# A four-layer conditional kernel: one identity add moved from VectorE to GpSimd, one load moved to ScalarE's queue, three warm-up matmuls fewer

## The reference

```
x = x + einsum('bct,bcd->bdt', x, W0[c15])        # L0: 16 matrices of 64 x 64, one picked per batch
x = x + einsum('bct,bcd->bdt', x, W1[c15])        # L1: the same form, the same condition
x = x + x @ W2.T + 0.5 * (x @ A[c2]) @ B.T        # L2: 1024 x 1024, with a low-rank part of rank 32
x = x + x @ W3[c7].T                              # L3: one of 8 matrices of 1024 x 1024 per batch
```

## Time and profile before

| | |
|---|---|
| runs | 385.03, 385.55, 385.63 us |
| the profiled execution's own time | 385.22 us |
| its span, from the first to the last instruction | 383.4 us |
| mean granted TensorE clock | 0.998 |
| TensorE busy | 377.7 us, 98% |
| VectorE busy | 269.2 us, 70% |
| ScalarE busy | 224.4 us, 59% |
| GpSimd busy | 117.8 us, 31% |

### The profile page before, as it was taken

How to read it: one execution, slowest core, us unless ns; L and a number is a source line. 1 busy time by engine, 2 the same in 40 slices (tenths; PEclk the granted TensorE clock), 3 DMA queues, 4 the chain that set the end, 5 groups by cost and what they waited for, 6 DMA issues and landing times.

```text
span 383.4 us, 7702 instructions
## 1 busy us (share of the span) xinstructions
PE 377.7 (98%) x1760; PEld 315.2 (82%) x1761; DVE 269.2 (70%) x300; ACT 224.4 (59%) x299; POOL 117.8 (31%) x157
## 2 busy tenths in 40 slices
PE   8999999999999999999999999999999999999995
PEld 8888888888888888888888888888888888888784
DVE  3796978856849788537869468963599626989643
ACT  3679558496246476245475465753677546778433
POOL 0000140100000000024766346753268532576500
PEclk9999999999999999999999999999999999999999
DMA  8975904640368384406427315552256522663223
GB/s 271 398 288 175 372 3 150 224 172 5 110 237 287 134 322 136 173 29 218 147 88 233 94 32 191 194 168 59 55 208 206 142 58 58 220 217 119 60 64 85
DMA packets 24187, 61.38 MB, mean 160 GB/s; under 512 B 1906, under 2 KB 2098, under 8 KB 24114
## 3 DMA queue, kind: packets, MB, share of 16 engines
q1 hardware_dynamic: 23792, 60.37, 47.3%
q10 hardware_dynamic: 322, 0.18, 0.2%
HBM read 52.15 MB, written 8.39 MB: 158 GB/s over the span
## 4 chain that ended last, share of the span: by engine, by line
PE 99%; POOL 0%; ACT 0%; issue 0%; ACTq 0%; POOLq 0%
PE ps L1496 45%; PE ps L1364 12%; PE ps L1363 12%; PE ps L1365 12%; PE ps L1390 4%; PE ps L1519 4%; PE ps L1429 3%; PE ps L1584 2%; PE ps L1402 2%; PE ps L1335 1%; PE ps L1343 1%; PE ps L1534 0%; POOL st L452 0%; ACT stage L841 0%; ACTq L840 0%
## 5 line engine op out<-in xcount | busy, mean ns | idle before, releaser
L1496 PE MATMUL ps<-ring,aT 128*128 x752 | 173.4, 389 | 0.0
L1496 PEld LDWEIGHTS ps<-ring,aT 128*128 128x128 f32 x752 | 141.0, 188 | 29.8 <-issue 0.7
L1364 PE MATMUL ps<-ring 128*128 128x512 f32 x208 | 81.0, 389 | 0.0
L1363 PE MATMUL ps<-ring 128*128 128x512 f32 x208 | 81.0, 389 | 0.0
L1365 PE MATMUL ps<-ring 128*128 128x512 f32 x208 | 80.9, 389 | 0.0
L471 POOL TENSOR_TENSOR aT<-xT,aT 128x512 fp32r<-128x512 f32 (+1 forms) x36 | 56.2, 1581 | 45.8 <-ACT aT L754 40.3
L1246 DVE TENSOR_TENSOR ring<-raw,ring 128x1024 f32 (+1 forms) x40 | 64.1, 1659 | 6.2 <-ACT ring L740 6.2
L760 ACT ACTIVATE aT<-ps 64x1024 fp32r<-64x1024 f32 x32 | 32.7, 1021 | 47.6 <-PE ps L1496 47.2
L1274 DVE TENSOR_TENSOR stage<-ps,stage 64x1024 f32<-64x1024 f32 x30 | 36.7, 1222 | 27.5 <-ACT stage L769 26.8
L1263 DVE TENSOR_TENSOR aT<-ps,aT 64x1024 fp32r<-64x1024 f32 x32 | 39.1, 1222 | 21.6 <-ACT aT L760 20.9
L1365 PEld LDWEIGHTS ps<-ring 128*128 128x128 f32 x208 | 39.0, 188 | 8.1
(11 more groups left out here) (94 smaller groups left out, 333.8 us busy)
## 6 DMA issues: line engine op xcount, KB each, us to landing
raw<-w3t SPq DMA_DIRECT2D x40, 512.0 KB, 4.3
ring_f<-xt SPq DMA_DIRECT2D x8, 1024.0 KB, 8.0
raw<-xt SPq DMA_DIRECT2D x8, 1024.0 KB, 5.3
out<-stage SPq DMA_DIRECT2D x30, 256.0 KB, 3.1
ring_f<-wt SPq DMA_DIRECT2D x4, 1024.0 KB, 7.8
xT<-xt SPq DMA_DIRECT2D x3, 1024.0 KB, 11.4
xT<-wt SPq DMA_DIRECT2D x2, 1024.0 KB, 16.2
ring_f<-wt SPq DMA_DIRECT2D x4, 256.0 KB, 5.2
```

Of the source, the lines that this page charges most:

```text
L1363: pe.matmul(dst, hi_of(qw)[:, k, cs], hi_of(qx)[:, k, :], start=start and k == 0, stop=False, skip_group_check=True)
L1364: pe.matmul(dst, hi_of(qw)[:, k, cs], lo_of(qx)[:, k, :], start=False, stop=False, skip_group_check=True)
L1496: last = pe.matmul(acc(i)[:, n, :], x3_split(i, k, start, P), ring[:, bass.ds(off + (part * D + n * 512), 512)], start=(k == 0 and j == 0) ...
```

## The change

The identity add of w1 goes from VectorE to GpSimd, with a semaphore of its own, `w1i`; VectorE's two adds for w0 count `w0i`. TensorE waits for both at c = 0. The load of x tile 0 goes from SyncE's queue, where it was fourth, to ScalarE's, where it is second, behind `eye`. WARM is 17.

```diff
-WARM, BRIDGE = 20, 6
+WARM, BRIDGE = 17, 6
@@ SyncE
                 sp.dma_start(raw_of(w_slot(0))[:, one, :], w_block(1, 1)[:, one, :]).then_inc(s(f"w_in0_{k}"), 16)
-                sp.dma_start(raw_of(x_slot(0))[:, one, :], x_block(1, 0)[:, one, :]).then_inc(s(f"x_in0_{k}"), 16)
+
+                if k:
+                    sp.dma_start(raw_of(x_slot(0))[:, one, :], x_block(1, 0)[:, one, :]).then_inc(s(f"x_in0_{k}"), 16)
@@ GpSimd
             pool.wait_ge(s("eye"), 16)
+            pool.wait_ge(s("w1"), 16)
+            v = w1_s.rearrange("p (c n) -> p c n", n=T)
+            pool.tensor_tensor(v, v, eye[:, P:P + T].unsqueeze(1).to_broadcast([P, NC_ // 2, T]), ALU.add).then_inc(s("w1i"), 1)
@@ ScalarE
             act.dma_start(eye[:, :], eye_c).then_inc(s("eye"), 16)
+            act.dma_start(raw_of(x_slot(0))[:, 0, :], xt[0, 1, 0]).then_inc(s("x_in0_0"), 16)
             act.dma_start(toks[:, :, :], indices).then_inc(s("toks"), 16)
@@ VectorE
-            dve.wait_ge(s("w1"), 16)
-            v = w1_s.rearrange("p (c n) -> p c n", n=T)
-            dve.tensor_tensor(v, v, eye[:, P:P + T].unsqueeze(1).to_broadcast([P, half, T]), ALU.add).then_inc(s("w01i"), 1)
             dve.wait_ge(s("w0"), 16)
...
-                   .then_inc(s("w01i"), 1)
+                   .then_inc(s("w0i"), 1)
@@ TensorE
             for c in range(NC_ // 2):
-                pe.wait_ge(s("w01i"), 2 if c < NC_ // 4 else 3)
+                if c == 0:
+                    pe.wait_ge(s("w1i"), 1)
+                pe.wait_ge(s("w0i"), 1 if c < NC_ // 4 else 2)
```

## The result

| | before | after |
|---|---|---|
| median | 385.27 us (384.74 to 385.91, 9 runs) | 387.70 us (386.39 to 388.76, 9 runs) |
| ratio | 1 | 1.0058, 95% interval 1.0041 to 1.0075 |
| the profiled execution | 385.22 us, span 383.4 | 388.76 us, span 387.0 |

The forecast was 385.6 (384.8 to 386.3), no change. The runs are 2.4 us slower, and they spread over 2.4 us where those of before spread over 1.2. The profiled one is the slowest of the nine, so its sum is to be held against its own 3.5 us and not against the median's 2.4.

What follows compares the result with a forecast made beforehand. TensorE, busy for 98% of the span, bounds the kernel, so P1's start decides: the later of 8.02 (table) and 8.05 us (x's high part), 0.1 later than 7.95. Forecast 385.6 us beside the median, range 384.8 to 386.3.

Steps and rivals of the forecast that it cites:

- the table's part: TensorE's table matmuls before P1: start at 5.98 us, end at 8.02 against 7.95, 0.07 us later than before.
- If the clock rises at 6.1 as before: TensorE's table: premise that the clock goes to 2.4 GHz at 6.1 us, so the table ends at 8.02.
- Rival 2: TensorE after the warm-up: clock rises late, at 10.73 us if the count restarts; 2.3 us lost, 387.9 us; chance 0.12.
- the pause is short beside 4.75: Argument against a late clock rise: TensorE's 0.84 us pause against the 4.75 us from first matmul to rise.
- The pause itself: TensorE between warm-up and table: idle from 5.14 to 5.98 us, 0.84 us.
- w1's add on GpSimd: Ahead of the table: starts at 3.92 us, takes 1.29, w1 ready at 5.21, at the latest 6.27.
- w0's halves behind GpSimd: VectorE's two adds ahead of the table: held by GpSimd until 5.21 us, ending at 5.89 and 6.49.
- w0's landing: Load ahead of the table: slowed some 0.5 us by x tile 0, landing at 4.4 to 4.95, costing nothing on top.
- The weight tile: Load ahead of P1: lands at 6.9 us instead of 5.8, x's high part ready at 7.97, P1 starting at 8.05.
- The pair is complete no sooner: Loads ahead of P1: weight tile 0 and x tile 0 together not there before 6.96 us, as before.
- Rival 1: Loads and port are kind: table starts at 5.30 us, ends at 7.59; gain 0.36 us, time 385.2; chance 0.22.
- P1 behind it: Tightest point after P1's start: x's low part for k = 1, ready at 11.31 us, wanted at 11.65; holds within 0.05.

Runs made afterwards that it cites:

- the first experiment: The kernel before with 17 warm-up matmuls instead of 20 and nothing else: 385.73 us, ratio 1.0028, six of twelve late.
- the filled table: The changed kernel, 17 warm-up matmuls, with seven full-size matmuls on zeros put between the table's c: 393.61 us, ratio 1.0189.

## Why the prediction was wrong

**The step that failed** is in the table's part: "If the clock rises at 6.1 as before". The whole sum stood on it. I read one profile and took its moment of rise for a property of the kernel. The experiments show the rise anywhere between 4.2 and 7.3 us in good profiles, and near 14 us (20 in one) or with a fall between in the late ones. The term of the sum that I had at zero, the longer stretch at the lower clock, measured 3.58 us in the profiled execution (1.64 in the table, 1.94 in P1). With the 20 matmuls back it is gone in eleven of twelve executions, so it is the three matmuls that I had counted as pure gain.

**Rival 2 named the clock**, with a chance of 0.12 and a price of 2.3 us; the medians give 2.4, but that it fits so well is luck. Its mechanism is that of the profiled execution and, by the granted clock, of three of the nine, and these lost 3.0 to 3.5 us. The median execution, and five of the nine, are by the same mark of the second form, where the clock rises in the warm-up and falls again; no rival had that. Its reason against, "the pause is short beside 4.75", was wrong. And its moment was wrong: in the profiled execution the rise did not come 4.75 us after the table's start at 6.21, at 11.0, but near 14.1, about 4.2 us after P1's start at 9.82 (2.9 to 5.6 us after it in the other profiles of this form). There the table of small matmuls did not do the warm-up's work. The pause itself was forecast nearly: from 5.14 to 5.98 us, and it lasted from there to 6.21. What the missing matmuls and the pause in their place do to the clock, I had put at nothing in the sum; the gain of 0.35 us does show in the profile of the first experiment.

**w1's add on GpSimd: right.** 1.27 us measured for 1.29. It began at 4.24 instead of 3.92, because `eye` landed later; that moment wanders (the first add starts at 3.9 to 4.5 us in the profiles, and at 4.2 to 4.3 in five of them without the moved load).

**w0's halves behind GpSimd: right in kind.** With w0 there at 4.6, VectorE's first half ended 0.56 us after GpSimd's add (6.05 and 5.49), for 0.68 forecast; in the change, where w0 was late, it took 0.90 instead of 0.68 and ended 0.56 us after GpSimd's add as well. What the Trainium skill says (SBUF — State Buffer, "Who interferes with whom"), that the second of two such instructions is blocked until the first is done, fits but for 0.12 us, by which the second ends sooner than its own 0.68 us after the first; the measurement decides.

**w0's landing: right, a little more than forecast.** 5.08 for "4.4 to 4.95". I said that it costs nothing on top, because GpSimd holds VectorE, and that held: without the moved load w0 landed at 4.6 and the table started at 6.19, with it at 5.08 and 6.21. The table's start is 0.23 us later than the forecast 5.98 because GpSimd ended 0.30 us later, at 5.51, behind `eye`; VectorE gave 0.12 back and the wait's release took 0.05 more.

**The weight tile: wrong.** It landed at 6.0, not 6.9. x's high part was ready at 7.09, before the table was done, so this term had no part in the result. "The pair is complete no sooner" was the wrong premise: both tiles were there by 6.0, before the change only by 6.96. The other loads did pay: beside the kernel without the moved load, w0 landed 0.5 us later and the rounding of the weight tile began at 6.05 instead of 5.51. That is what the Trainium skill says (DMA: Bandwidth & Descriptors, "Issuing engines are not separate DMA queues"), that loads issued from several engines interleave on the same DMA engines; the price of 1.1 us for the weight tile was mine. Rival 1 read idle capacity out of the 0.04 MB that SyncE's queue moved between 4.6 and 5.0 us, but the same row gives its packets a share of 99.8%; what made room for x is not shown.

**P1 behind it: right.** Nothing in P1 was late; all of its 1.9 us is pace.

## What to carry to other kernels

A warm-up is not filler that may be cut to the moment when the operands come. Before cutting it, ask what TensorE does between its end and the next unbroken full-size work, pauses and small matmuls taken together, and what it costs if the clock is down there: up to 3.5 us against the 0.2 us of each matmul saved. A moment of the clock read from one profile is one draw; run a kernel a dozen times and count the groups before calling a fraction of a per cent a gain.

## What the hardware showed that was not expected

- The rise of the clock wanders by some 3 us (4.2 to 7.2 us) between executions of kernels whose first warm-up matmul starts at 1.35 us: 20 warm-up matmuls took 3.89 us in one profile and 4.63 in another.
- Once up, it can fall again soon: up in the warm-up, 0.50 from 8.0 to 11.4 us while P1 ran without a pause from 8.22 on. In the profile with 18 matmuls it fell at 8.3 us, when P1 had been running for 0.3 us, and with the table moved behind P1 1.4 us into P1.
- Seven full-size matmuls strewn among 16 small ones left TensorE at 1.2 GHz from the start to about 20 us in the profile.
- In the profile of the change the granted clock is printed as 1.00 from 10 to 14 us although the matmuls last 628 ns for 389; in that of GpSimd's add without the moved load the same durations stand beside 0.50. Durations show the clock in both, the column only in one.
- An add on VectorE behind one on GpSimd ended 0.55 to 0.56 us after it in six profiles (the change; with 20, 19 and 18 matmuls; with the filled table; without the moved load), whether w0 had landed at 4.6 or at 5.5 us.
